# A transformer layer on eight cores: a projection moved ahead in attention, and the down projection in one pass with two weight buffers

## The reference

```python
q_nope, q_pe = q[..., :128], q[..., 128:]          # q = rmsnorm(xn @ w_q_a) @ w_q_b
q_abs  = einsum('bshd,rhd->bshr', q_nope, w_uk)    # into the 512-wide latent space
q_full = concat([q_abs, rope(q_pe)]); k_full = concat([ckv, rope(k_pe)])
scores = einsum('bqhd,bkd->bhqk', q_full, k_full) * sm_scale    # causal mask
o_ckv  = einsum('bhqk,bkr->bqhr', softmax(scores), ckv)
y      = einsum('bqhr,hre->bqe', o_ckv, w_o_abs)   # w_uv and w_o
```

## Time and profile before

| | us |
|---|---|
| median of 2 runs | 7747.24 |
| lowest, highest | 7741.88, 7752.59 |
| the profiled execution | 7760.94 |
| its span, slowest core (core 6) | 7759.2 |
| spans of the 8 cores | 7698.9 to 7759.2 |

### The profile page before, as it was taken

How to read it: one execution, slowest core, us unless ns; L and a number is a source line. 1 busy time by engine, 2 the same in 40 slices (tenths; PEclk the granted TensorE clock), 3 DMA queues, 4 the chain that set the end, 5 groups by cost and what they waited for, 6 DMA issues and landing times. The chain is left out here.

```text
span 7759.2 us, 71053 instructions; the slowest of 8 cores (7698.9 to 7759.2 us)
## 1 busy us (share of the span) xinstructions
PE 5462.6 (70%) x24385; PEld 2406.7 (31%) x24856; DVE 1792.9 (23%) x4772; ACT 1200.6 (15%) x2756; POOL 365.2 (5%) x408
## 2 busy tenths in 40 slices
PE   3355545566666666666667689975998599859994
PEld 1122222222222222223222234432443244324442
DVE  3323333313331333313333310011001100110001
ACT  0000012212222232313333210000000000000000
POOL 0000011111111100000000000000000000000000
PEclk7676766677778888888888899997999799979997
DMA  4321169987678464362333257854786479546864
GB/s 94 83 48 24 24 90 135 125 125 96 82 90 121 61 78 67 63 115 46 59 59 59 48 117 185 206 147 129 172 218 161 117 166 233 142 128 153 236 153 115
DMA packets 2182741, 886.91 MB, mean 114 GB/s; under 512 B 1823347, under 2 KB 2142964, under 8 KB 2180342
## 3 DMA queue, kind: packets, MB, share of 16 engines
q1 hardware_dynamic: 1703222, 694.32, 36.5%
q0 software_dynamic: 479168, 188.02, 21.1%
HBM read 921.31 MB, written 148.90 MB: 138 GB/s over the span
## 5 line engine op out<-in xcount | busy, mean ns | idle before, releaser
L1011 PE MATMUL ps<-fx,wg 128*128 128x512 bf16 x4014 | 925.8, 381 | 139.2 <-DMA fx<-xnt_scr 115.8
L1019 PE MATMUL ps<-fx,wg 128*128 128x512 bf16 x4015 | 919.6, 379 | 4.3
L756 PE MATMUL ps<-kT,qf 128*128 128x512 bf16 (+3 forms) x2482 | 716.9, 421 | 291.0 <-DVE qf L683 175.2
L1076 PE MATMUL ps<-wd,h_sb 128*128 128x512 bf16 x2007 | 468.4, 395 | 338.1 <-DVE os L1115 331.1
L824 PE MATMUL ps<-ptasm,ckv_nat 128*128 128x512 bf16 (+3 forms) x2511 | 612.6, 414 | 75.1 <-DVE ptasm L717 74.3
L706 PE MATMUL pt<-ident_sb,p_nat 128*128 128x128 bf16 x2176 | 228.9, 271 | 570.0 <-DVE ptasm L717 472.1
L1011 PEld LDWEIGHTS ps<-fx,wg 128*128 128x128 bf16 x4096 | 401.9, 98 | 624.6 <-issue 147.2
L1034 DVE TENSOR_TENSOR h_sb<-sil,ps 128x512 bf16<-128x512 f32 x256 | 176.0, 688 | 1717.3 <-PE ps L1019 1717.3
L1019 PEld LDWEIGHTS ps<-fx,wg 128*128 128x128 bf16 x4096 | 400.8, 98 | 483.3
L792 ACT ACTIVATE p_nat<-s_stage,e_bias 128x512 bf16<-128x512 f32 (+3 forms) x640 | 414.2, 648 | 617.2 <-DVE e_bias L787 617.2
L1029 ACT ACTIVATE sil<-ps 128x512 f32<-128x512 f32 x256 | 152.8, 597 | 2227.9 <-PE ps L1011 2227.9
(11 more groups left out here) (106 smaller groups left out, 3347.2 us busy)
## 6 DMA issues: line engine op xcount, KB each, us to landing
wg<-wgup_bf SPq DMA_DIRECT2D x512, 512.0 KB, 4.6
wd<-wdown_bf SPq DMA_DIRECT2D x384, 512.0 KB, 6.5
conv<-wgup POOLq DMA_DIRECT2D x128, 512.0 KB, 10.5
wgup_bf<-conv SPq DMA_DIRECT2D x128, 512.0 KB, 11.0
wo<-wo POOLq DMA_DIRECT2D x16, 2048.0 KB, 21.6
conv<-wdown POOLq DMA_DIRECT2D x64, 512.0 KB, 9.2
wdown_bf<-conv SPq DMA_DIRECT2D x64, 512.0 KB, 7.8
wnope<-wqbnope POOLq DMA_DIRECT2D x64, 384.0 KB, 16.8
```

What stands on the lines that cost most here:

```text
L756: lhs=lhs, rhs=rhs: e.matmul(bank[:, 0:w], lhs(e), rhs(e), start=(cc == 0), stop=(cc == 4)),
L1011: b.op("tensor", lambda e, gs=gs, ec=ec, s_g=s_g, pg=pg: e.matmul(pg[:, :], wg_sb[s_g][:, ec * 128:(ec + 1) * 128], xnt_g[gs][:, ec * 512: ...
L1019: b.op("tensor", lambda e, gs=gs, ec=ec, s_u=s_u, pu=pu: e.matmul(pu[:, :], wg_sb[s_u][:, ec * 128:(ec + 1) * 128], xnt_g[gs][:, ec * 512: ...
L1076: slot=slot, banks=banks: e.matmul(banks[tt4][:, :], h_sb[:, ic * 512 + tt4 * 128:ic * 512 + (tt4 + 1) * 128], wd_sb[slot][:, i4 * 512:(i4 ...
```

## The change

Attention. The 12 `wnope` matmuls with the weight load and the ACT copy behind them become a function, `emit_qnope`. It is called for head 0 at the start of a block; for head h + 1 it is called within head h, behind the transposes of tile 2 and ahead of those of tile 3. The load of `wnope` for head h + 2 is issued there too.

Down projection. Pass A, `ybufA` and its evictions are gone. All 64 `ic` of an `eg` run in one go after step 63, in banks 2 to 5, 256 matmuls per `eg`. The down weights have two buffers instead of eight; the tile for the next four `ic` is requested at the start of the present four (across the ends of `eg` and g too), so that its load waits for the four before. A token group makes 64 loads. At the end of an `eg`, ACT copies the four banks to a new buffer `ydn_sb`, which frees the banks; DVE adds xr + yr and then ydn, and SP stores. `xr` and `yr` are loaded once per token group, right behind `fx`, as eight DMAs of 1 MB. All `wd` loads keep their place in the program's order, so the second tile of an `eg` is requested behind the `out` stores of the `eg` before.

```diff
+                def emit_qnope(h2, B=B, d_qat=d_qat):
+                    hs2 = h2 % 2
+                    b.waits("tensor", [d_nope[hs2], d_qat, ps_free[5]])
+                    for lc in range(12):
+                        b.op("tensor", lambda e, hs2=hs2, lc=lc: e.matmul(
+                            PS[5][:, :], wnope_sb[hs2][:, lc * 128:(lc + 1) * 128],
...
+                    if h2 < 15:
+                        load_nope(h2 + 1, 1 - hs2)
+                    elif B < NB - 1:
+                        load_nope(0, 1 - hs2)
+                    wnope_free[hs2] = (T, t_qn)
+                    b.waits("scalar", [(T, t_qn), qnope_free[hs2]])
+                    s_qn = b.op("scalar", lambda e, hs2=hs2: e.copy(
+                        qnope_sb[hs2][:, :], PS[5][:, :]), Sc)
...
+                for h in range(16):
+                    hs = h % 2
+                    emit_conversions(3)
+                    if h == 0:
+                        s_qn_tok[0] = emit_qnope(0)
+                    s_qn = s_qn_tok[hs]
...
                         pend_tr = (i, n_k, v_pn)
+                    if h < 15:
+                        s_qn_tok[1 - hs] = emit_qnope(h + 1)
                     emit_transposes(*pend_tr)
...
-            wd_sb = [psb(f"wd{i}", [128, 4 * 512], BF16) for i in range(8)]
-            ybufA = psb("ybufA", [128, 16 * 512], F32)
+            wd_sb = [psb(f"wd{i}", [128, 4 * 512], BF16) for i in range(2)]
-            xr_sb = [psb(f"xr{i}", [128, 512], F32) for i in range(2)]
-            yr_sb = [psb(f"yr{i}", [128, 512], F32) for i in range(2)]
+            xr_sb = psb("xr_sb", [128, 16 * 512], F32)
+            yr_sb = psb("yr_sb", [128, 16 * 512], F32)
+            ydn_sb = psb("ydn_sb", [128, 4 * 512], F32)
...
+                b.waits("sync", [xr_free, yr_free, ya_done[g]])
+                for tt4 in range(4):
+                    d_xr = SQ.dma(lambda e, g=g, tt4=tt4: e.dma_start(
+                        xr_sb[:, tt4 * 2048:(tt4 + 1) * 2048],
+                        x_d[g * 512 + tt4 * 128:g * 512 + (tt4 + 1) * 128, :]))
+                    d_yr = SQ.dma(lambda e, g=g, tt4=tt4: e.dma_start(
+                        yr_sb[:, tt4 * 2048:(tt4 + 1) * 2048],
+                        ya_scr[g * 512 + tt4 * 128:g * 512 + (tt4 + 1) * 128, :]))
...
-                    if 31 <= j <= 45 and (j - 31) % 2 == 0:
-                        passA_emit((j - 31) // 2, h_half, ybufA_free, pa_pend,
-                                   pa_frees)
...
                 for eg in range(4):
+                    if g == 0 and eg == 0:
+                        load_down(0, 0, 0)
...
+                    for ic in range(64):
+                        isl = (ic // 4) % 2
+                        if ic % 4 == 0:
+                            nic = ic + 4
+                            neg, ng2 = eg, g
+                            if nic >= 64:
+                                nic = 0
+                                neg = eg + 1
+                                if neg >= 4:
+                                    neg, ng2 = 0, g + 1
+                            if ng2 < 4:
+                                load_down(neg, nic, 1 - isl)
+                        b.waits("tensor", [d_d[isl]])
+                        for tt4 in range(4):
...
+                        if ic % 4 == 3:
+                            wd_free[isl] = (T, b.cnt[T])
                     t_dn = b.cnt[T]
+                    b.waits("scalar", [(T, t_dn), ydn_free])
                     for tt4 in range(4):
-                        xsl = tt4 % 2
-                        b.waits("sync", [xr_free[xsl]])
...
+                        b.op("scalar", lambda e, tt4=tt4, banks=banks: e.copy(
+                            ydn_sb[:, tt4 * 512:(tt4 + 1) * 512],
+                            banks[tt4][:, :]), Sc if tt4 == 3 else None)
+                    s_dn = b.cnt[Sc]
+                    for k in range(4):
+                        ps_free[2 + k] = (Sc, s_dn)
+                    for tt4 in range(4):
                         osl = tt4 % 2
+                        b.waits("vector", [d_xr, d_yr, (Sc, s_dn),
                                            out_free[osl]])
...
+                    v_cmb = b.cnt[V]
+                    ydn_free = (V, v_cmb)
+                    if eg == 3:
+                        xr_free = (V, v_cmb)
+                        yr_free = (V, v_cmb)
```

More of the change, by code:

```diff
@@ L655, in build_nc @@
                     t_qn = b.cnt[T]
-                    if h < 15:
-                        load_nope(h + 1, 1 - hs)
+                    if h2 < 15:
+                        load_nope(h2 + 1, 1 - hs2)
                     elif B < NB - 1:
[L659 to L663, removed]
-                    ps_free[5] = (Sc, s_qn)
+                        load_nope(0, 1 - hs2)
[3 more added lines that the diff above has]
+                        qnope_sb[hs2][:, :], PS[5][:, :]), Sc)
+                    ps_free[5] = (Sc, s_qn)
+                    return s_qn
+                s_qn_tok = [None, None]
+                for h in range(16):
[4 more added lines that the diff above has]
+                    s_qn = s_qn_tok[hs]
                     qab_banks = (3, 4, 5, 0)
@@ L926, in build_nc @@
             wg_free = [None] * 4
-            wd_free = [None] * 8
-            ybufA_free = None
-            wd_rr = [0]
+            wd_free = [None, None]
             sil_free = [None, None]
-            xr_free = [None, None]
-            yr_free = [None, None]
+            xr_free = None
+            yr_free = None
+            ydn_free = None
+            d_xr = None
+            d_yr = None
             out_free = [None, None]
@@ L935, in build_nc @@
             d_g = [None] * 4
-            d_d = [None] * 8
+            d_d = [None, None]
             out_dma = None
@@ L942, in load_gate_tile, with load_down @@
                 d_g[slot] = SQ.dma((lambda oc, slot: _dma3(wg_sb[slot], wgup_bf[oc, :, :, :], 128))(oc, slot))
-            def load_down(eg, ic0):
-                slot = wd_rr[0] % 8
-                wd_rr[0] += 1
+            def load_down(eg, ic0, slot):
                 b.waits("sync", [wd_free[slot]])
[L948 to L987, removed]
@@ L1068, in build_nc @@
                             + [ps_free[2 + k] for k in range(4)])
[L1069 to L1083, removed]
+                    for ic in range(64):
[12 more added lines that the diff above has]
+                        for tt4 in range(4):
+                            b.op("tensor", lambda e, ic=ic, tt4=tt4, isl=isl,
+                                 banks=banks: e.matmul(
+                                     banks[tt4][:, :],
+                                     h_sb[:, ic * 512 + tt4 * 128:ic * 512 + (tt4 + 1) * 128],
+                                     wd_sb[isl][:, (ic % 4) * 512:(ic % 4 + 1) * 512],
+                                     start=(ic == 0), stop=(ic == 63)),
+                                 T if (tt4 == 3 and ic % 4 == 3) else None)
+                        if ic % 4 == 3:
+                            wd_free[isl] = (T, b.cnt[T])
@@ L1111, in build_nc @@
                                         ALU.add), V)
-                        ya_reads.append((V, v_o2))
-                        b.wait("vector", V, v_o2)
-                        v_ob = b.op("vector", lambda e, osl=osl, tt4=tt4, banks=banks:
-                                    e.tensor_tensor(
-                                        out_sb[osl][:, :], out_sb[osl][:, :],
-                                        banks[tt4][:, :], ALU.add), V)
-                        ps_free[2 + tt4] = (V, v_ob)
@@ L1119, in build_nc @@
-                        xr_free[xsl] = (V, v_ob)
-                        yr_free[xsl] = (V, v_ob)
                         b.wait("sync", V, v_ob)
```

54 lines of the change are left out of this document (9 added, 45 removed).

## The result

The changed kernel is faster: the ratio to the kernel before is 0.9581, 95% interval 0.9559 to 0.9603. On the scale of the first runs (7747.24 us) that is 7423 us.

A forecast was written before the change was run, and what follows sets the result against it. TensorE work was taken as the bound, so removing its idle time shortens the kernel. Terms -187 - 30 - 192 - 19 + 69 + 40 + 51 = -268 took 7760.9 to 7493, 7480 us on the median's scale; 8-in-10 range 7350 to 7640.

The forecast's parts named there:

- burst: Token group's start: eight 1 MB xr/yr loads take 40 us and delay gate tiles; 40 lost first, 51 at later groups.
- moved chain: Attention: q_nope matmuls leave the head's start for the gap before the last transposes, 60 heads; 187 us gained.
- clock in attention: Attention: a filled gap may raise TensorE's clock, against slower scores; 30 us gained, bounds 0 and 100.
- ends of output groups: Down projection: TensorE idle per output group falls from 29.4 to 13.4 us, twelve times; 192 us gained.
- the kernel's own end: From the last matmuls' end to the last store: shortens from 29 us to 10, 19 us gained.
- stall per weight tile: Down projection, two weight buffers: 0.33 us per tile over 212 tiles, 69 us lost; bounds 48 and 345.
- (a): Rival, down projection: weights land late, near the 6.5 us median; 345 instead of 69 lost, total 7755; chance 0.15.
- (b): Rival, down projection: small stalls let the clock fall to 1.2 GHz; 770 lost, total about 8250; chance 0.07.
- (c): Rival, attention: the scores' stage runs slower and gives back some 2 us per head, 120 us; total 7600; chance 0.08.
- (d): Rival, more gain: attention's clock 70 more, quicker xr/yr loads 28, down weights landing in 3.7 us 21; 7361; chance 0.10.

The follow-up runs named there:

- Experiment 3: The kernel before with twelve extra, unread matmuls in the gap ahead of the last transposes of heads 0 to 14, nothing moved; ratio 0.9904.
- experiment 4: The changed kernel with three weight buffers instead of two, each tile requested two ahead; ratio 0.9428, lowest execution 7273.65 us.
- Experiment 6: The changed kernel with the eight xr and yr loads issued one at a time behind weight tiles of gate steps; ratio 0.9499, lowest 7356.49 us.

## Why the prediction was right or wrong

The forecast took 268 us off the profiled execution; its span lost 330 (237 in attention, 91 in the feed-forward stage, 3 before). On the scale of the first runs 7423 us stand against the forecast's 7480. In direction and mechanism every step stood. Two failed in size: the price of the `xr`/`yr` burst, the largest error, and the clock's share in attention, the one that nothing offset. That the feed-forward stage came out near its forecast on the mean of the cores (64 us gained, 51 forecast) is in part luck: the burst's error is offset by those of the stall and of the output groups' ends. The terms in us (+ is time lost), measured from the matmuls' starts as time above 0.216 us per matmul; attention is the mean of the eight cores, the rest that of the six whose matmul records are complete (1 to 5 and 7):

| term | forecast | measured |
|---|---|---|
| moved chain | -187 | -187 |
| clock in attention | -30 | -68 |
| ends of output groups | -192 | -174 |
| the kernel's own end | -19 | -15 |
| stall per weight tile | +69 | +106 |
| burst | +91 | +33 |
| small waits in pass A and the gate steps | 0 | -7 |
| sum | -268 | -312 |

The mean of all eight spans fell by 320 us; the 8 us between come from cores 0 and 6, which are left out of the lower five rows.

**The moved chain (187): right.** From the start of L850 to that of L669 a head now needs 0.86 us instead of 4.4 in blocks 1 to 3; the gap grew by 1.66 us in block 0 and 0.17 in block 1, where 1.6 and 0.3 were put down. 3.58 x 60 - 15 x 1.83 = 187.

**The clock in attention (30, bounds 0 and 100): the second step that failed.** The step took the middle between a gain at the attention products and a loss at the scores. Of attention's 255 us, 187 are the moved chain; 68 are left for this term, and not 30. The products gained 1.94, 1.11 and 0.53 us per head, 54 us; the last transposes and the `ptasm` copy behind them some 13; and block 0, where all of the head's start had run slower, another 10 (5.11 - 0.86 is 4.25 and not 3.58); some 9 came back elsewhere, 6 of them because the first scores start 0.1 us later. The scores' stage gave back nothing clear: -0.6, +0.5 and +0.2 us in blocks 1 to 3. Experiment 3 shows that the filled gap does this by itself, 52 us. The trace alone could have said more: the earlier trace rows has the products at half speed behind an idle gap, and nothing there spoke for a loss of the same size.

**The end of an output group (192): right on the core it was read from.** 2.46 + 8.56 + 2.3 = 13.4 us per boundary on core 3, where 13.4 were forecast; the 19 us at the kernel's end were 16. The 29.4 us of before are those of core 6; on the mean of the six cores it was 28.0, and 13.5 after, so the term is 174.

**The stall per weight tile (69): the mechanism right, the size not.** The periods on core 3 exceed 3.45 us by 114 us over the 212 tiles, 0.54 each and not 0.33. L was well chosen: nearly alone in flight, loads land in 3.6 to 4.1 us (the whole kernel's median is 3.8):

```profile
DMA to landing us min/median/max: 3.6/3.7/4.1
```

That is the landing of the loads issued from 4900 to 4950 us. What was too small is the 0.2 us that stand beside L in the sum, for wake-ups alone. In the rows of experiment 4 two tiles take about 7.9 us; less 3.45 of matmuls and 3.7 to 3.8 of landing, some 0.7 us are left for them and for waits that a late load hands on to the next tile. How these divide was not measured.

**The burst (91): the step that failed most.** It took the rate from a lone 1 MB load, 210 GB/s. Queued one behind the other, the loads move much faster. Bytes moved in the changed kernel from 5125 to 5145 us:

```profile
DMA packets 2961, 7.54 MB, mean 377 GB/s; under 512 B 2104, under 2 KB 2104, under 8 KB 2104
```

At that rate the eight take 22 us and not 40; from packet to packet of this burst the eight cores moved 339 to 415 GB/s. The start lost 38.9 - 15.7 = 23 us instead of 40. At the group boundaries 20.7 us for `fx` and 13.6 for `wg` stand where 38.95 were, the answer to the earlier trace rows:

```profile
5112.90 0.64 SPq L121 DMA_DIRECT2D fx<-xnt_scr  x1
...
5123.27 6.11 PE L988 MATMUL ps<-fx,wg 128*128 128x512 bf16 x16 [20.83 <-DMA fx<-xnt_scr]
...
5146.45 4.00 PE L988 MATMUL ps<-fx,wg 128*128 128x512 bf16 x9 [13.61 <-DMA wg<-wgup_bf]
```

Core 6, from which the 38.95 were read, waited longest; on the other cores it was 33 to 37 us. With the two slow restarts a boundary of token groups costs 3 to 4 us more than before on the mean of the cores, and not 17 more. The term measured 22 us at the start and 11 at the three boundaries, 33 us, 58 less than the 91. Experiment 6, in which the burst is gone from these places, gains 65 us, as against the 64 that its waits on core 3 come to. The rule of the Trainium skill that the prediction used ("DMA: Bandwidth & Descriptors", section "Bandwidth": batches of 1 MiB or more reach at least 75% of peak), which the lone load didn't bear out, gave an estimate of 25 us; for the queued loads the trace agrees with it, at 377 GB/s. The other figure from the Trainium skill (the same page, section "Anatomy of one DMA — SWDGE (gpsimd) path", an estimate of 3.2 us for 512 KB) stays too low for these loads, which SP issues: on no core of the changed kernel did a load of `wd` land in less than 3.4 us.

**The rivals.** (a), loads landing late, did not happen: 3.8 us. (b), the clock falling in the down projection, did not: the 32-matmul runs above last 7.07 us, full speed, with a stall at every second tile. (c) and the thought behind it, that the scores pay for the hoist, fell. (d) is nearest to what happened, but in other sizes: the clock gave 38 us more (70 said), the burst cost 58 less (28 said), and the weight loads cost 37 more instead of 21 less.

## What to carry to other kernels

Size a double-buffered load by (work + landing + wake-ups) / number of buffers and not by whether landing is shorter than the work: here one more buffer of 512 KB was worth about 150 us, because landing (3.8 us) exceeded the work (3.45). Ask of every load what stands ahead of it on its queue: a request behind stores that wait for another engine, or behind a burst that nobody needs yet, costs TensorE time although its data is ready to move. And price an idle gap on TensorE by what the matmuls behind it lose in speed, too: work that fills it can be worth more than its own length (in blocks 0 and 1 it was, in block 3 it gave nothing).

## What the runs showed of the hardware that I had not expected

- Adding 720 matmuls of 128x512, read by nobody, made the kernel about 1% faster (ratio 0.9904), since the products behind them ran at 2.4 and not 1.2 GHz (2.33 instead of 4.42 us for 16).
- A lone 1 MB load with 8 KB rows moved at 210 GB/s; eight of them in one queue at 377 GB/s, in a stage in which every core of the chip loads the same way (339 to 415 GB/s on the eight cores).
- A stall of 0.5 to 1 us at every second weight tile did not lower the clock: from 4890 to 4945 us the granted clock was 0.97.
